# Transformer block on one core: value bias added in the copies, first pair of heads without sums, and another order of the sync queue

## The reference

```python
Q, K, V = x @ W.T + b, per head; Q, K rotated
scores = where(causal, Q @ K.T / sqrt(32), -inf)
out = softmax(scores) @ V @ Wo.T + bo
x = x + attn(layernorm(x))
g, u = (x_n @ gate_w.T) * gate_s, (x_n @ up_w.T) * up_s
x = x + (silu(g) * u) @ down_w.T * down_s
```

## Time and profile before

| | us |
|---|---|
| median of 3 runs (lowest, highest) | 749.34 (746.14, 752.66) |
| the profiled execution | 753.23 |
| its span, first to last instruction | 751.5 |
| PE busy | 725.0 |
| DVE, ACT, POOL busy | 456.9, 318.3, 367.3 |

### The profile page before, as it was taken

How to read it: one execution, slowest core, us unless ns; L and a number is a source line. 1 busy time by engine, 2 the same in 40 slices (tenths; PEclk the granted TensorE clock), 3 DMA queues, 4 the chain that set the end, 5 groups by cost and what they waited for, 6 DMA issues and landing times.

```text
span 751.5 us, 12585 instructions
## 1 busy us (share of the span) xinstructions
PE 725.0 (96%) x4427; PEld 555.6 (74%) x4427; DVE 456.9 (61%) x1103; ACT 318.3 (42%) x657; POOL 367.3 (49%) x331
## 2 busy tenths in 40 slices
PE   7999999998999999999999999999999999999995
PEld 7787888766666666665666568878788888888884
DVE  6979683987888888887888535953243125114113
ACT  3231323255676776665666662222332232222221
POOL 0627383737768686757667617812232223223222
PEclk9999999998999999999999999999999999999998
DMA  8584659644667677766667385930000001001001
GB/s 280 179 271 181 229 214 284 253 157 142 173 166 211 181 201 188 208 184 175 185 184 197 83 234 179 371 142 1 0 21 36 0 1 56 0 0 56 1 1 58
DMA packets 55382, 106.74 MB, mean 142 GB/s; under 512 B 14788, under 2 KB 18372, under 8 KB 54804
## 3 DMA queue, kind: packets, MB, share of 16 engines
q1 hardware_dynamic: 55320, 105.95, 45.5%
HBM read 69.88 MB, written 38.21 MB: 144 GB/s over the span
## 4 chain that ended last, share of the span: by engine, by line
PE 72%; DVE 8%; DMA 7%; issue 7%; SPq 2%; POOL 2%; ACT 1%; DVEq 0%; POOLq 0%; ACTq 0%
PE ps L1225 29%; PE ps L1366 13%; PE ps L1464 9%; PE ps L1250 9%; PE ps L1343 9%; DMA q_st<-neg_T 3%; DMA xr<-in_x 2%; DMA x_st<-in_x 2%; PE ps L1217 1%; POOL hid_lo L696 1%; PE ps L1284 1%; DVE x L1135 1%; DVE xn L902 1%; DVE stats L887 1%; DVE xst_c L902 1%
## 5 line engine op out<-in xcount | busy, mean ns | idle before, releaser
L787 ACT ACTIVATE p<-ps 128x384 f32<-128x384 f32 (+3 forms) x384 | 162.8, 492 | 30.7 <-PE ps L1343 29.8
L1343 PE MATMUL ps<-q_st,k_st 99*128 99x384 f32 (+2 forms) x384 | 138.9, 369 | 4.0 <-DMA q_st<-neg_T 2.6
L696 POOL TENSOR_TENSOR hid_lo<-hid,hid_hi 128x512 fp32r<-128x512 f32 x44 | 56.7, 1289 | 174.0 <-ACT hid_hi L874 174.0
L959 DVE CUSTOM_DVE_ANT_0 masked<-ps,mask_qk 128x512 bf16<-128x512 f32 (+1 forms) x240 | 113.7, 503 | 42.8 <-PE ps L1250 41.1
L1250 PE MATMUL ps<-k_st,q_st 96*128 96x512 f32 (+2 forms) x384 | 132.3, 366 | 6.0 <-DVE row_max L959 4.6
L1176 DVE SCALAR_TENSOR_TENSOR hid<-ps,us_sb,silu 128x512 f32<-128x512 f32 x44 | 33.1, 751 | 165.8 <-PE ps L1225 159.5
L1366 PE MATMUL ps<-p,v_slot 128*32 128x256 f32 (+2 forms) x1512 | 119.8, 379 | 0.3 <-ACT o_raw L801 0.3
L1366 PEld LDWEIGHTS ps<-p,v_slot 128*32 128x32 f32 (+1 forms) x1512 | 62.7, 116 | 53.0 <-issue 22.1
L1343 PEld LDWEIGHTS ps<-q_st,k_st 99*128 99x128 f32 x384 | 73.3, 192 | 25.7 <-issue 9.5
L1250 PEld LDWEIGHTS ps<-k_st,q_st 96*128 96x128 f32 x384 | 73.8, 193 | 24.6 <-DVE row_max L959 11.6
L961 DVE TENSOR_REDUCE row_max<-ps 128x1 f32<-128x512 f32 (+1 forms) x128 | 81.1, 649 | 0.8 <-PE ps L1250 0.3
(11 more groups left out here) (130 smaller groups left out, 1266.7 us busy)
## 6 DMA issues: line engine op xcount, KB each, us to landing
qk_scratch<-st_hi SPq DMA_DIRECT2D x32, 512.0 KB, 3.8
...
flag_st<-in_ffn SPq DMA_DIRECT2D x32, 264.0 KB, 2.9
ffn_copy<-in_ffn SPq DMA_DIRECT2D x32, 264.0 KB, 3.3
...
```

Source lines behind the costliest of these rows:

```text
L696: pool.tensor_tensor(hid_lo[:, i % 3, :], hid[:, i % 2, :], hid_hi[:, i % 3, :].bitcast(F32), ALU.subtract).then_inc(hid_lo_done, 1)
L787: act.activation(p32[:, at:at + q0 + w - keep], ps[:, ST_BANK + i % ST_RING, keep - q0:w], ACT.Exp, scale=SCALE).then_inc(exp_done, 1)
L959: ins = dve.tensor_tensor_reduce((masked_a if u < 2 else masked)[:, s_before(i) % 2, col:col + kept], scores, mask_qk[:, 512 - kept:512], ...
L1343: pe.matmul(ps[:, ST_BANK + i % ST_RING, 0:w], k_st[0:K_ALL, slot, kt * P:(kt + 1) * P], q_st[0:K_ALL, slot, q0:q0 + w], start=True, stop= ...
```

## The change

Four edits. (1) The value bias is no longer added to `v_sb` by POOL in sixteen tiles of 128x512; `copy_v` adds it while it copies the head's 128x256 values, so the copy becomes an addition with two inputs. (2) Pair 0 uses the products without sums, as the last pair does; steps 0 and 1 have no `sum_p`, and pairs 0 and 15 move no `o_w`. (3) SP issues the rows of maxima, then the test load and copy, and only then the moves of both heads of a pair; `store_rec` also comes behind the test load and copy. (4) DVE forms the reciprocals behind piece 6 of the step, not behind piece 2; POOL adds `o_w` in its own step (`join_group`, t % 4 == 3, behind `mask_low`) and `scale_group` follows `mask_low`. There is one `o_w` buffer, not two, and the moves of an even pair wait for the join of the group before.

```diff
-            def add_value_bias(n):
-                ...
-                pool.tensor_tensor(v_sb[:, b, kt, :], v_sb[:, b, kt, :], bv_sb[:, :], ALU.add).then_inc(v_biased, 1)
...
             def copy_v(t):
                 b, h = divmod(t, NH)
-                pool.wait_ge(v_biased, TJ * CC * (b + 1))
+                pool.wait_ge(v_ready, TJ * CC * (b + 1))
...
-                pool.tensor_copy(v_slot[:, t % SLOTS, :, 0:D], v_sb[:, b, :, h * D:(h + 1) * D]).then_inc(v_copied, 1)
+                cols = slice(h * D, (h + 1) * D)
+                pool.tensor_tensor(v_slot[:, t % SLOTS, :, 0:D], v_sb[:, b, :, cols], bv_sb[:, cols].unsqueeze(1).to_broadcast([P, KT, D]),
+                                   ALU.add).then_inc(v_copied, 1)
...
+            def join_group(g):
+                for k in range(2):
+                    pool.wait_ge(o_moved[k], moved(k, g + 1))
+                rows = slice(2 * D if g == 0 else 0, 4 * D)
+                ...
+                pool.tensor_tensor(o_T[rows, g, S // 2:S], o_T[rows, g, S // 2:S], o_w[rows, :], ALU.add).then_inc(o_joined, 1)
...
             def scale_group(g):
                 pool.wait_ge(rec_in, 64 * (g + 1))
-                pool.tensor_tensor(o_T[:, g, S // 2:S], o_T[:, g, S // 2:S], o_w[g % 2][:, :], ALU.add).then_inc(o_joined, 1)
                 pool.wait_ge(o_joined, g + 1)
...
             for t in range(HEADS):
                 copy_v(t)
+                mask_low(t)
                 if t % 4 == 0 and t >= 8:
                     scale_group((t - 8) // 4)
-                mask_low(t)
-                if t < HEADS - 2:
+                if t % 4 == 3 and t >= 7:
+                    join_group((t - 7) // 4)
+                if t // 2 not in PLAIN:
                     sum_p(t)
                 mask_high(t)
-                if t < TJ:
-                    add_value_bias(TJ * (N_CH - 1) + t)
```

```diff
-                if t % 2 == 0 and t >= 4:
-                    move_pair((t - 4) // 2, (0,))
                 if t + 1 < HEADS:
                     load_max(t + 1)
-                if t % 2 == 0 and t >= 4:
-                    move_pair((t - 4) // 2, (1,))
-                if t % 4 == 3 and t >= 7:
-                    store_rec((t - 7) // 4)
-                ...
                 cols = slice(t * FFN_PIECE, (t + 1) * FFN_PIECE)
                 ...
                 sp.dma_start(flag_st[:, :], ffn[:, cols]).then_inc(flag_in, 16)
                 sp.dma_start(ffn_copy[:, cols], ffn[:, cols]).then_inc(ffn_copied, 16)
+                if t % 2 == 0 and t >= 4:
+                    move_pair((t - 4) // 2)
+                if t % 4 == 3 and t >= 7:
+                    store_rec((t - 7) // 4)
                 ...
-                    if t % 4 == 3 and t >= 7 and i == 2:
+                    if t % 4 == 3 and t >= 7 and i == 6:
                         reciprocals((t - 7) // 4)
...
-PV_TAIL = [
+PLAIN = (0, PAIRS - 1)
+PV_PLAIN = [
...
-                part, rounds = (PV_TAIL if u == PAIRS - 1 else PV_GROUPS)[group]
+                part, rounds = (PV_PLAIN if u in PLAIN else PV_GROUPS)[group]
...
-                    if u < PAIRS - 1:
-                        pe.wait_ge(p_summed, 2 * u + 2)
+                    if u not in PLAIN:
+                        pe.wait_ge(p_summed, 2 * u)
```

59 lines of the change are left out of this document (30 added, 29 removed).

## The result

| | before | changed |
|---|---|---|
| median, us (executions) | 749.11 (20) | 745.89 (20) |
| lowest to highest | 744.89 to 757.48 | 740.99 to 749.68 |
| the profiled execution | 753.23 | 743.76 |
| its span | 751.5 | 742.0 |

The ratio of the changed kernel to the one before is 0.9944, with a 95% interval of 0.9922 to 0.9965: 3.2 us less on the medians, some 4 us by the ratio; within 1%, but a difference and not none. The two profiled executions are 9.5 us apart, three times the difference of the medians; where those 9.5 us lie has to be read with that in mind.

A forecast was written before the change was run, and what follows sets the result against it. PE, busy 725.0 of 751.5 us, was taken as the bound. Step 1 -1.0, pair 0 +0.7, queues 0 and POOL 0 sum to -0.3 us, a median of 749.0 us, range 743.0 to 755.5.

The forecast's parts named there:

- the likeliest case: Whole kernel: the forecast of -0.3 us, median 749.0 us, with its own range 746.5 to 751.5; chance 0.45.
- rival A: SP's queue: the moves were the blockage, long pairs and waits go, -9.1 us; whole or in part 741 to 746.5, chance 0.25.
- Step 1: Start of stage B: without POOL's bias tile DVE's test and PE's wait shorten; -1.0 us, ends 0.5 and 3.0.
- Pair 0: First pair of stage B: products without sums keep PE busy longer; +0.7 us, bounds 0.5 to 1.0.
- Queues: SP's DMA order in stage B: maxima gain 1.4 us, the later store costs 1.1; taken as 0 for the six groups.
- the later of my two ends: Store of reciprocals on SP: it waits for the copy in HBM and lands at 297.9 us; the other end is 297.0.
- the two falls of the clock at 345 and 417 stay: Stage B: the two drops of PE's clock to about half rate, in the two pairs over 20 us, remain after the change.
- by bytes that is 196 of 1476 KB: DMA queues ahead of the rows of maxima: one head's moves as a share of the bytes, worth 1.4 us.
- POOL: Stage B: the copy as an addition and the moved join and scaling cost zero on PE's path.
- rival C: DVE's test in step 1 or later: POOL's new addition or join still meets it; 750.0 to 751.3 us, chance 0.10.
- B: Stage B: late reciprocal store makes heads' loads late in six groups; +12.0 us, 761.3; whole or in part over 752, chance 0.20.
- keys named as often as maxima: Check at the end of steps t % 4 == 0: PE's waits name head keys as often as maxima, sum 2 to 4 us.

The follow-up runs named there:

- e1: Changed kernel with SP's old order of moves, rows of maxima and store, and reciprocals behind piece 2 again; 749.21 us, ratio 1.0033.
- e6: Changed kernel with a plain copy in place of the addition, the value bias left out of the result; 743.96 us, ratio 0.9914.
- e2: Changed kernel with POOL's sixteen bias tiles, the plain copy and the sums of pair 0 put back; 746.00 us, ratio 0.9966.
- e4: Changed kernel with the store of reciprocals ahead of the test load and copy, reciprocals behind piece 4; 744.92 us, ratio 0.9945.
- e5: Changed kernel with POOL's scaling cut into two halves, in steps t % 4 == 0 and 1; 741.06 us, ratio 0.9905.
- e3: Changed kernel with only the moves of a pair's first head put ahead of the rows of maxima again; 749.91 us, ratio 1.0011.
- e9: e5 with DVE's test in steps t % 4 == 1 behind piece 9 instead of piece 4; 749.68 us, ratio 1.0004.
- r1: The changed kernel measured again, unchanged, on one chip beside the version with the scaling in halves; 744.19 us, ratio 0.9940.
- e10: Changed kernel with the sums of pair 0 put back, the bias still added in the copy; 745.02 us, ratio 0.9938.

## Why the prediction was right, and where it was not

By its bounds it held: 745.9 lies in 743.0 to 755.5, and "within 1%" came true. But the range is 12.5 us wide, and the number came out right more by that width than by the reasoning. The forecast of -0.3 us was measured as -3.2, and -0.3 us, a ratio of 0.9996, lies outside the measured interval. 745.9 is just under the likeliest case's own range of 746.5 to 751.5, in the one given to rival A (741 to 746.5). And by its own last sign, "wrong as a whole if pairs of more than 20 us are gone", the prediction was wrong: the longest pair of the changed kernel is 18.9 us. That sign was a poor one, though. e1, with the old queue and as slow as before, has no pair over 19.0 us in its profiled execution, and e6, with the new queue, has one of 20.03. By its steps:

**Step 1, -1.0 (0.5 to 3.0).** Right in mechanism and to the hundredth in its first part: test 1.90 to 0.90, wait 1.94 to 0.94. Whether the clock stays up, which I left open, is open in fact. The eleven kernels with the new start all wait 0.93 or 0.94 us. From the test to the second pair they then take 23.4 or 23.5 us (two of them, without a fall), 25.0 (four), or 26.0 to 26.7 (five). Before and e2 take 26.1 and 26.3. The mean of the eleven is 25.3, 0.9 under the old start, of which there are only these two executions. Stretches right behind the wait, of e1_old_queue:

```profile
165.90:172.70 6.80, 6.77 (x20) 0.52 0.68 199
```

and of the changed kernel:

```profile
167.50:174.30 6.80, 6.80 (x37) 1.00 0.67 201
```

**Pair 0, +0.7 (0.5 to 1.0).** The term was too small. In the changed kernel pair 0 takes 18.27 us and pair 1 17.09; e4 and e5 have 18.28 and 18.28 for it, so it costs +1.2. L1373 is busy 8.65 us there, not 8.0. The last pair, from which I took 7.99, has the same 72 products but was not a fair measure of the first. Since the stretch of the last paragraph contains pair 0, its -0.9 is the net of both: step 1 alone gave about -2.1. Both terms were too small, with opposite signs, and the net is -0.9 where -0.3 was forecast.

**Queues, 0.** This is the step that failed. The store's own landing was at the later of my two ends, with the reloads 3.02 us behind it, but what follows from it was mis-sized twice. The heads' keys are issued 2.7 us later in the step (-0.6 to 2.1 in the table), where I had 0.9 to 1.8 and took 1.1. And their way got 2.0 us shorter (7.3 to 5.3), where I had let only the rows of maxima gain, by 1.4 us. About 1.0 of these 2.0 come with the moves (e1 to e4) and 0.9 with the late store (e4 to changed), whose delay I had booked as a pure loss. The net is keys that land 0.7 us later in the step. The Trainium skill, DMA: Bandwidth & Descriptors, Queues, rings and completion order, has a semaphore increment land only after every earlier write of its DMA engine; with the copy in HBM ahead the median landing is 3.3 us, with the store ahead of it 2.2 (e4), so the trace agrees. And a head's keys were waited for, 2.4 us in all. The waits of the changed kernel for transfers are 2.4 us where they were 3.0, so as a balance of waits the zero was nearly right. What failed is the sentence behind it, "the two falls of the clock at 345 and 417 stay". The waits for maxima went, and so did the two falls. e3 shows the worth of the place of the moves: 3.9 us more waits for transfers, two falls, and +4.0 us in the median. That is more than the 1.4 us of "by bytes that is 196 of 1476 KB". e1, with both edits put back, is at +3.3 us in the median.

That the order on SP decides about a fall is not shown, only that the kernels with the old order or e3's are slower over their executions. Behind the second pair, the fourteen profiled executions have two falls in before, two in e3, one each in e6 and e9, both of which have the new order, and none in the other ten, e1 among them. Falls followed waits of 1.05 us and of 0.36 and 0.76 us (before), 0.53 and 0.52 us and 1.39 and 0.32 us (e3), 1.33 us (e6) and 1.36 us (e9). None followed 1.26 and 0.48 us (e3), 1.14 us and 1.31 us (changed), 1.21 us (e1) and six waits of 1.02 to 1.06 us (e4). What tells the two sets apart, no run here shows.

**POOL, 0.** It failed too, and I had the tool in hand: "PE never waited for POOL in stage B" is true of both kernels and says nothing of DVE. The scaling behind the mask pushes the sums into DVE's test in steps t % 4 == 1, at about 1.05 us of PE's time in four to six places. e5 shows that 3 us of the rest of B come back when the meeting is taken away. It is the mechanism of rival C, which I had tied to the addition in the copy and to the join; e6 clears the one. That the scaling ahead of the mask, without the join, would do as well as halves was not tried.

**The sum.** Averaged over the four kernels that have the new queue and POOL's new places behind the second pair (changed, r1, e2, e10: 228.4, 227.8, 227.2, 227.2), the rest of B is 227.7 against 230.3: -2.6, made of a gain by the moves and a loss by the scaling. (e2 has the plain copy as well.) With -0.9 for the start this is -3.5, near the measured -3.2. The value for before is one execution with two falls of the clock in it, so the agreement is partly luck. A good part of the gain is the clock: over its executions the changed kernel was granted 0.993 on the mean (0.994 in r1), the one before 0.990 to 0.991, e1 and e3, which gain nothing, both 0.990. 0.002 to 0.003 of 746 us are 1.5 to 2.2 us of the 3.2. But the clock is not the whole: e9 was granted 0.994 and gains nothing, by its longer waits.

**Stage A, not in the sum.** The bias tiles of stage A I had called worth nothing. PE's wait for `ocos` before stage B is 1.3 us before and 2.8 in e2, both with tiles, and nothing to 1.5 us in the twelve without. The start of stage B is at 126.9 and 129.6 with them, at 122.5 to 126.6 without. This points to a further gain, but e2's median, 746.0, is hardly above the changed kernel's, so it is not shown.

**Rivals.** A was true in what it said of the blockage: the long pairs are gone (the two at these places take 18.9 and 18.8 us) and no fall is left. It was wrong in price, since two waits for keys and four for DVE took the place. B's store came at its 3.0 us, beyond the 2.3 that I had named as the point of decision, and B did not happen: PE waited for keys at two heads, not six. The table of landings says why: the way of the keys shortened by 2.0 us while their issue moved back by 2.7. Of my checks, "keys named as often as maxima" missed (all keys, no maxima), and L1373 was not "about 8.0 us" but 8.65. The reloads, forecast as 0.9 to 1.8 us later behind the test copy, go 3.6 us behind it in step 15, where they went 0.9 behind it: 2.7 later. The sum of the waits for transfers, 2 to 4 us, held.
